# Node stage of a graph layer on one core: the residual term formed by GpSimd and copied into PSUM by ScalarE instead of transposed in by TensorE

## The chip, the cores and the metric

The kernel runs on one core of a Trainium2 chip. The metric is the device time of one execution in microseconds (us). The kernel before was timed three times: 1971.91, 1972.24 and 1974.71 us, median 1972.24.

Five engines are named in what follows: TensorE (PE, and PEld for its weight loads), VectorE (DVE), ScalarE (ACT), GpSimd (POOL) and SyncE (SP, which issues DMAs).

## The reference, cut to what matters

x has 50000 rows of 256, there are 12500 edges and 8 heads. The change lies in the part after the attention.

```python
h = maximum(layernorm(x), 0)                      # row by row
out = attention over the edges, of h              # other stages; their result + Wo_b is the table "agg"
out = layernorm(h + out, ln1_g, ln1_b)            # "zn * g1 + b1", zn without gain and shift
ffn = gelu(out @ ffn_w1 + ffn_b1) @ ffn_w2 + ffn_b2
out = layernorm(out + ffn, ln2_g, ln2_b)
return x + out
```

All is float32. Products of the feed-forward part are made from split operands: each factor is a high part (rounded to the fast matmul type f32r) and a low part (the rest), and three of the four products are summed.

## The kernel before

Four stages run one after the other: scores of the edges, softmax, messages, and the node stage (function `node_stage`), which is the one that changes. The node stage takes the rows in NG = 98 groups of GR = 512 rows, GT = 4 tiles of 128 rows each. KD = 2 halves of the 256 features, KF = 4 quarters of the 512 hidden features. Each engine has its program written out for all groups: a loop over `s` from -6 to NG, in which every engine does, in a fixed order, a part of the work of group s and parts of groups before and after it. Semaphores tie the engines together; an engine works strictly in its own order.

TensorE, step s: F, the first product, quarter by quarter (c = 0 to 3, six matmuls of 512 columns each, L904, f32r) into two PSUM banks in turn; then eight transposes of `ut` into the banks of Y (L912), which start the accumulation with the residual term; then eight transposes of `zn` of group s+1 into T (L923, T has two banks); then the second product, 48 matmuls of 256 columns (L931), into the same Y.

ScalarE, step s: `zn` of group s+1 (L819), gelu of each quarter from PSUM into `act_full` in SBUF (L850), its high part `act_hi` (L856), the first layer's normalisation `z` of group s+4 (L819), the high part `zt_hi` of T (L874, 1024 elements), and `ut = g1 * T + (b1 + fb2)` (L879, twice 512 elements).

VectorE, step s: for group s-1, once its second product is done, statistics of Y (L760, four), their aggregation (L763, four) and the centring of Y (L779, four); then `low_part(s, 0)` (L768: `act_lo = act_full - act_hi`), statistics of z of group s+2, `low_part` 1 and 2, the output of group s-1 (L797, four), `low_part` 3, `zt_lo` of group s+1 (L805), statistics of x of group s+5. In front of each aggregation stands `hold`: a wait for the statistics and an increment of another semaphore.

GpSimd, step s: the DMA that adds `agg` to z of group s+3 (L722) and one that adds a constant to x (L724), then the small scale factors of x (s+4), of y (s-1) and of z (s+2) (L707 to L715), each with a power (L711) of 128x4. SyncE loads x (L681) and stores the result (L687).

TensorE waits for: `lo_done` (all of `zt_lo` of its group) before F; `gelu_done` of quarter c-2 before F of quarter c; `ut_done` and `o_done` before L912; `zn_done`, `lo_done` and `ut_done` before L923; `glo_done` (the low part of quarter c) before quarter c of the second product.

Of the kernel before, what the change touches and what calls it, by code (L numbers as in the profile page):

```python
# [18 lines left out]
P = 128  # L19
KD = D // P  # L20
KF = F // P
# [584 lines left out]
def node_stage(nc, x, given, w1, w2, out, agg_dram):  # L606

    with ExitStack() as ctx:
# [15 lines left out]
        res_col = sb("d_res_col", [P, KD])  # L624
        ident = sb("d_ident", [P, P])
        mhalf = sb("d_mhalf", [P, GT])
        xt = [sb(f"d_x{r}", [P, GT, D]) for r in range(XR)]
        z = [sb(f"d_z{r}", [P, GT, D]) for r in range(ZR)]
        zn = [sb(f"d_zn{r}", [P, GT, D]) for r in range(2)]
        zt_hi, zt_lo = sb("d_zt_hi", [P, KD, GR], f32r), sb("d_zt_lo", [P, KD, GR], f32r)  # L630
        act_full = sb("d_act", [P, KF, GR])
        act_hi, act_lo = sb("d_act_hi", [P, KF, GR], f32r), sb("d_act_lo", [P, KF, GR], f32r)
        ut = sb("d_ut", [P, KD, GR])
        o = [sb(f"d_o{r}", [P, GT, D]) for r in range(2)]
        norm = {n: dict(stats=sb(f"d_stats_{n}", [P, NR, GT, 6]), mv=sb(f"d_mv_{n}", [P, NR, GT, 2]),
                        veps=sb(f"d_veps_{n}", [P, NR, GT]), rstd=sb(f"d_rstd_{n}", [P, NR, GT]),
                        nmean=sb(f"d_nmean_{n}", [P, NR, GT]), nmr=sb(f"d_nmr_{n}", [P, NR, GT]), stats_done=sem(f"d_stats_done_{n}"),
                        mv_done=sem(f"d_mv_done_{n}"), veps_done=sem(f"d_veps_done_{n}"),
                        rstd_done=sem(f"d_rstd_done_{n}"), nmr_done=sem(f"d_nmr_done_{n}")) for n in "xzy"}
# [3 lines left out]
        w_in, consts, prep, bias_ps = sem("d_w_in"), sem("d_consts"), sem("d_prep"), sem("d_bias_ps")  # L643
        x_in = [sem(f"d_x_in{r}") for r in range(XR)]
        b2_in = [sem(f"d_b2_in{r}") for r in range(XR)]
        agg_in = [sem(f"d_agg_in{r}") for r in range(ZR)]
        stored = [sem(f"d_stored{r}") for r in range(2)]
        h_done, zn_done = sem("d_h_done"), sem("d_zn_done")
        t_done, hi_done, lo_done = sem("d_t_done"), sem("d_hi_done"), sem("d_lo_done")
        f_done, gelu_done, ghi_done, glo_done = sem("d_f_done"), sem("d_gelu_done"), sem("d_ghi_done"), sem("d_glo_done")  # L650
        ut_done = sem("d_ut_done")
        ffn_done, centred, o_done = sem("d_ffn_done"), sem("d_centred"), sem("d_o_done")
        passed, pool_passed = sem("d_passed"), sem("d_pool_passed")
# [4 lines left out]
                   (res_col, v["fb2_col"]))  # L658
        N_IN = 16 * (2 + len(vectors))
        FIRST, LAST = -6, NG + 1  # L660
        PREP = 8

        def rows_of(table, g):

            at = g.times(GR) if g.i is not None or g.c < NG - 1 else N - GR
            return table[bass.ds(at, GR), :].rearrange("(p j) d -> p j d", j=GT)

        with nc.Block() as block:
            @block.sync
            def _(sp):  # L670
                sp.dma_start(w1_raw[:], w1.rearrange("(k p) n -> p k n", p=P)).then_inc(w_in, 16)
                sp.dma_start(w2_raw[:], w2.rearrange("(k p) n -> p k n", p=P)).then_inc(w_in, 16)
                for to, of in vectors:
                    sp.dma_start(to[:], of).then_inc(w_in, 16)  # L674

                def step(s):
                    g = s + 6
                    if g.exists(NG):
                        if g.after(XR):
                            sp.wait_ge(o_done, g.times(1, 1 - XR))  # L680
                        sp.dma_start(xt[g.c % XR][:], rows_of(x, g)).then_inc(x_in[g.c % XR], 16)  # L681
                    g = s + -1
                    if g.exists(NG):
                        sp.wait_ge(o_done, g.times(1, 1))
                        if g.i is None and g.c == NG - 1:
                            sp.wait_ge(stored[(g.c - 1) % 2], (g + -1).use(2, 16))
                        sp.dma_start(rows_of(out, g), o[g.c % 2][:]).then_inc(stored[g.c % 2], 16)  # L687
                for s in range(FIRST, LAST):
                    step(Step(s))
                for r in range(2):  # L690
                    sp.wait_ge(stored[r], 16 * ((NG + 1 - r) // 2))

            @block.gpsimd
            def _(pool):
                nc.gpsimd.memset(ident[:], 0.0).then_inc(consts, 1)
                nc.gpsimd.memset(mhalf[:], -0.5).then_inc(consts, 1)
                pool.wait_ge(consts, 2)
# [4 lines left out]
                def scales(n, g):  # L702

                    q, r = norm[n], g.c % NR
                    hold(pool, q["mv_done"], g.times(1, 1), pool_passed)
                    if n != "y":
                        nc.gpsimd.tensor_scalar(q["nmean"][:, r], q["mv"][:, r, :, 0], -1.0, 0.0, ALU.mult, ALU.add)  # L707
                    nc.gpsimd.tensor_scalar(q["veps"][:, r], q["mv"][:, r, :, 1], 1.0, LN_EPS, ALU.mult, ALU.add)\
                        .then_inc(q["veps_done"], 1)
                    pool.wait_ge(q["veps_done"], g.times(1, 1))  # L710
                    nc.gpsimd.tensor_tensor(q["rstd"][:, r], q["veps"][:, r], mhalf[:], ALU.pow)\  # L711
                        .then_inc(q["rstd_done"], 1)
                    if n != "y":
                        pool.wait_ge(q["rstd_done"], g.times(1, 1))
                        nc.gpsimd.tensor_tensor(q["nmr"][:, r], q["nmean"][:, r], q["rstd"][:, r], ALU.mult)\  # L715
                            .then_inc(q["nmr_done"], 1)

                def step(s):
                    g = s + 3
                    if g.exists(NG):  # L720
                        pool.wait_ge(h_done, g.times(1, 1))
                        pool.dma_start(z[g.c % ZR][:], rows_of(agg_dram, g), accum_op=ALU.add)\  # L722
                            .then_inc(agg_in[g.c % ZR], 16)
                        pool.dma_start(xt[g.c % XR][:], b2_wide[:], accum_op=ALU.add).then_inc(b2_in[g.c % XR], 16)  # L724
                    g = s + 4
                    if g.exists(NG):
                        scales("x", g)
                    g = s + -1
                    if g.exists(NG):
                        scales("y", g)  # L730
                    g = s + 2
                    if g.exists(NG):
                        scales("z", g)
                for s in range(FIRST, LAST):
                    step(Step(s))

            @block.vector
            def _(dve):
# [16 lines left out]
                done(nc.vector.tensor_tensor(res_col[:], res_col[:], b1_col[:], ALU.add))  # L755

                def statistics(name, g, t):
                    q, r = norm[name], g.c % NR
                    for j in range(GT):
                        nc.vector.bn_stats(q["stats"][:, r, j, :], t[:, j, :]).then_inc(q["stats_done"], 1)  # L760
                    hold(dve, q["stats_done"], g.times(GT, GT), passed)
                    for j in range(GT):
                        ins = nc.vector.bn_aggr(q["mv"][:, r, j, :], q["stats"][:, r, j, :])  # L763
                    ins.then_inc(q["mv_done"], 1)

                def low_part(s, c):
                    dve.wait_ge(ghi_done, s.times(KF, c + 1))
# [3 lines left out]
                def step(s):  # L771
                    y = s + -1
                    q, yr, yn = norm["y"], y.c % 2, y.c % NR
                    if y.exists(NG):
                        dve.wait_ge(ffn_done, y.times(1, 1))
                        statistics("y", y, Y[yr])
                        dve.wait_ge(q["mv_done"], y.times(1, 1))
                        for j in range(GT):
                            nc.vector.scalar_tensor_tensor(Y[yr][:, j, :], Y[yr][:, j, :], q["mv"][:, yn, j, 0:1],  # L779
                                                           g2_row[:], ALU.subtract, ALU.mult).then_inc(centred, 1)  # L780
                    if s.exists(NG):
                        low_part(s, 0)
                    g = s + 2
                    if g.exists(NG):
                        dve.wait_ge(agg_in[g.c % ZR], g.use(ZR, 16))
                        statistics("z", g, z[g.c % ZR])
                    if s.exists(NG):
                        low_part(s, 1)
                        low_part(s, 2)
                    if y.exists(NG):  # L790
                        dve.wait_ge(q["rstd_done"], y.times(1, 1))
                        dve.wait_ge(b2_in[y.c % XR], y.use(XR, 16))
                        dve.wait_ge(centred, y.times(GT, GT))
                        if y.after(2):
                            dve.wait_ge(stored[yr], (y + -2).use(2, 16))
                        for j in range(GT):
                            ins = nc.vector.scalar_tensor_tensor(o[yr][:, j, :], Y[yr][:, j, :], q["rstd"][:, yn, j:j + 1],  # L797
                                                                 xt[y.c % XR][:, j, :], ALU.mult, ALU.add)
                        ins.then_inc(o_done, 1)
                    if s.exists(NG):  # L800
                        low_part(s, 3)
# [194 lines left out]
```

## Time and profile before

The profiled execution took 1970.92 us, of which 1969.2 us lie between its first and its last instruction.

| | busy us | share of the span | instructions |
|---|---|---|---|
| PE | 1767.6 | 90% | 10564 |
| PEld | 1498.4 | 76% | 10564 |
| DVE | 1503.4 | 76% | 4348 |
| ACT | 1278.4 | 65% | 2290 |
| POOL | 1046.1 | 53% | 1645 |

The node stage takes the span from about 624 us on; its first F matmul starts at 672.36 us and the last instructions of group 97 end the execution. The profile cuts the span into 40 slices and gives each engine's busy tenths in them; the second row is TensorE's granted clock in tenths of full speed.

```profile
PE   0999999729892499999999999999999999999997
PEclk9999999959896699999999999999999999999999
```

From the fifteenth slice on PE is busy for nine tenths or more. Busy says that a matmul was under way, not that the engine was at its peak. The chain that ended last is followed back from the last instruction, and names at each step what released it.

```profile
PE 66%; DVE 1%; POOL 1%; DMA 0%; ACT 0%; issue 0%; SPq 0%; DVEq 0%; POOLq 0%; ACTq 0%
```

### The profile page before, as it was taken

Reading aid. Unit: us, or ns where it says so; the run is one execution under the profiler, and the core shown is the slowest. Engines: PE = TensorE matmul, PEld = TensorE weight load, DVE = VectorE, ACT = ScalarE, POOL = GpSimd, SP = SyncE. Lnnn points to the kernel's source line nnn. Section 1 sums busy time; section 2 is a strip of 40 time slices with the busy share of each in tenths; the row PEclk is TensorE's granted clock in tenths of the full one; section 3 lists DMA queues with packets and bytes.
Section 4 is the critical chain, followed back from the end, with each engine's and each line's share of the span. In section 5 each row is a group of like instructions: output and inputs, shape, how many; then the busy total and the mean of one; then the engine's idle time right before and its main releaser. Section 6 shows DMA issues by size and latency. Waiting matters only on the chain.

```text
span 1969.2 us, 32889 instructions
## 1 busy us (share of the span) xinstructions
PE 1767.6 (90%) x10564; PEld 1498.4 (76%) x10564; DVE 1503.4 (76%) x4348; ACT 1278.4 (65%) x2290; POOL 1046.1 (53%) x1645
## 2 busy tenths in 40 slices
PE   0999999729892499999999999999999999999997
PEld 0666666516561399999999999999999999999997
DVE  2554554357671599999999999999999999999986
ACT  1666666400000588888888888888888888888884
POOL 6777776006773555555555555555555555555541
PEclk9999999959896699999999999999999999999999
DMA  3677677402333667766776667666766676667651
GB/s 100 222 236 243 216 247 234 150 30 79 109 119 105 144 154 160 169 160 157 159 171 157 158 158 171 158 156 159 172 158 157 158 171 159 158 156 171 160 120 43
DMA packets 131718, 308.26 MB, mean 157 GB/s; under 512 B 13917, under 2 KB 67851, under 8 KB 131569
## 3 DMA queue, kind: packets, MB, share of 16 engines
q0 software_dynamic: 42624, 139.33, 33.2%
q1 hardware_dynamic: 36800, 114.52, 19.7%
q10 hardware_dynamic: 52144, 52.56, 8.4%
q8 instruction: 76, 1.25, 0.3%
q14 instruction: 74, 0.60, 0.1%
HBM read 139.98 MB, written 117.79 MB: 131 GB/s over the span
## 4 chain that ended last, share of the span: by engine, by line
PE 66%; DVE 1%; POOL 1%; DMA 0%; ACT 0%; issue 0%; SPq 0%; DVEq 0%; POOLq 0%; ACTq 0%
PE d_Y L931 29%; PE d_F L904 28%; PE d_Y L912 4%; PE d_T L923 4%; DMA d_res_col<-in_fb_col 0%; ACT d_z L819 0%; POOL d_rstd_x L711 0%; POOL d_x L724 0%; PE d_F L889 0%; SPq L674 0%; DVE d_Y L779 0%; DVE d_stats_y L760 0%; DVE d_stats_x L760 0%; POOL d_z L722 0%; DVE d_o L797 0%
## 5 line engine op out<-in xcount | busy, mean ns | idle before, releaser
L931 PE MATMUL d_Y<-d_w_hi,d_act_hi 128*128 128x256 f32 x1568 | 451.2, 288 | 0.0
L931 PE MATMUL d_Y<-d_w_lo,d_act_hi 128*128 128x256 f32 x1568 | 443.0, 283 | 0.0
L931 PE MATMUL d_Y<-d_w_hi,d_act_lo 128*128 128x256 f32 x1568 | 439.4, 280 | 0.0
L819 ACT ACTIVATE d_z<-d_x,d_nmr_x,d_rstd_x 128x256 f32<-128x256 f32 x392 | 223.9, 601 | 253.6 <-POOL d_nmr_x L715 253.6
L850 ACT ACTIVATE d_act<-d_F,d_fb_col 128x512 f32<-128x512 f32 x392 | 266.9, 681 | 145.1 <-PE d_F L904 144.9
L904 PE MATMUL d_F<-d_zt_hi,d_w_hi 128*128 128x512 f32 x784 | 311.8, 398 | 3.3 <-DVE d_zt_lo L805 3.3
L904 PE MATMUL d_F<-d_zt_lo,d_w_hi 128*128 128x512 f32 x784 | 311.6, 397 | 0.0
L904 PE MATMUL d_F<-d_zt_hi,d_w_lo 128*128 128x512 f32 x784 | 311.0, 397 | 0.0
L931 PEld LDWEIGHTS d_Y<-d_w_hi,d_act_lo 128*128 128x128 f32 x1568 | 298.4, 190 | 0.0
L931 PEld LDWEIGHTS d_Y<-d_w_hi,d_act_hi 128*128 128x128 f32 x1568 | 294.5, 188 | 0.0
L931 PEld LDWEIGHTS d_Y<-d_w_lo,d_act_hi 128*128 128x128 f32 x1568 | 293.3, 187 | 0.0
L768 DVE TENSOR_TENSOR d_act_lo<-d_act,d_act_hi 128x512 fp32r<-128x512 f32 x392 | 257.2, 676 | 6.3 <-ACT d_act_hi L856 6.3
L856 ACT ACTIVATE d_act_hi<-d_act 128x512 fp32r<-128x512 f32 x392 | 244.7, 624 | 0.3
L819 ACT ACTIVATE d_zn<-d_z,d_nmr_z,d_rstd_z 128x256 f32<-128x256 f32 x392 | 222.2, 593 | 0.0
L760 DVE BATCH_NORM_STATS2 d_stats_y<-d_Y 128x6 f32<-128x256 f32 x392 | 139.7, 419 | 79.3 <-PE d_Y L931 79.3
L879 ACT ACTIVATE d_ut<-d_T,d_res_col,d_g_col 128x512 f32<-128x512 f32 x196 | 142.0, 775 | 87.1 <-DVE d_zt_lo L805 87.1
L707 POOL TENSOR_SCALAR d_nmean_z<-d_mv_z 128x4 f32<-128x4 f32 x98 | 42.1, 430 | 276.0 <-DVE d_mv_z L763 276.0
L904 PEld LDWEIGHTS d_F<-d_zt_hi,d_w_lo 128*128 128x128 f32 x784 | 148.0, 189 | 36.1
L904 PEld LDWEIGHTS d_F<-d_zt_hi,d_w_hi 128*128 128x128 f32 x784 | 148.1, 189 | 35.6 <-DVE d_zt_lo L805 3.7
L904 PEld LDWEIGHTS d_F<-d_zt_lo,d_w_hi 128*128 128x128 f32 x784 | 148.0, 189 | 31.2
L779 DVE SCALAR_TENSOR_TENSOR d_Y<-d_Y,d_mv_y,d_g_row 128x256 f32<-128x256 f32 x392 | 163.3, 485 | 3.5
L722 POOL DMA_DIRECT2D d_z<-agg_scratch x98 | 91.2, 930 | 134.8 <-ACT d_z L819 134.8
(147 smaller groups left out, 3634.9 us busy)
## 6 DMA issues: line engine op xcount, KB each, us to landing
agg_scratch<-a_bias_row ACTq DMA_DIRECT2D x50, 1024.0 KB, 6.5
d_x<-in_x SPq DMA_DIRECT2D x98, 512.0 KB, 5.3
d_z<-agg_scratch POOLq DMA_DIRECT2D x98, 512.0 KB, 7.4
d_x<-d_b_wide POOLq DMA_DIRECT2D x98, 512.0 KB, 9.2
out<-d_o SPq DMA_DIRECT2D x98, 512.0 KB, 2.9
c_cont<-cont_scratch SPq DMA_DIRECT2D x25, 256.0 KB
a_xd<-in_x,a_idx_now POOLq DMA_INDIRECT x100, 6.1
a_xs<-in_x,a_idx_now POOLq DMA_INDIRECT x100, 2.9
```

Of the source, the lines that this page charges most:

```text
L722: pool.dma_start(z[g.c % ZR][:], rows_of(agg_dram, g), accum_op=ALU.add)\
L760: nc.vector.bn_stats(q["stats"][:, r, j, :], t[:, j, :]).then_inc(q["stats_done"], 1)
L768: nc.vector.tensor_tensor(act_lo[:, c, :], act_full[:, c, :], act_hi[:, c, :].bitcast(f32), ALU.subtract).then_inc(glo_done, 1)
L779: nc.vector.scalar_tensor_tensor(Y[yr][:, j, :], Y[yr][:, j, :], q["mv"][:, yn, j, 0:1], g2_row[:], ALU.subtract, ALU.mult).then_inc(centr ...
L819: return nc.scalar.activation(to[:, j, :], of[:, j, :], func, bias=q["nmr"][:, r, j:j + 1], scale=q["rstd"][:, r, j:j + 1])
L850: nc.scalar.activation(act_full[:, c, :], FF[:, c % 2, :], ACT.Gelu, bias=fb1_col[:, c:c + 1])\
L856: nc.scalar.activation(act_hi[:, c, :], act_full[:, c, :], ACT.Identity).then_inc(ghi_done, 1)
L879: nc.scalar.activation(ut[:, k, :], T[:, k, :], ACT.Identity, bias=res_col[:, k:k + 1], scale=g1_col[:, k:k + 1]).then_inc(ut_done, 1)
L904: ins = nc.tensor.matmul(FF[:, c % 2, :], w[:, k, c * P:(c + 1) * P], a[:, k, :], start=(k == 0 and p == 0), stop=(k == KD - 1 and p == 2))
L912: nc.tensor.matmul(out[:, j, k * P:(k + 1) * P], ut[:, k, j * P:(j + 1) * P], ident[:], is_transpose=True, start=(j % 2 == 0 and k == 0), ...
L923: ins = nc.tensor.transpose(T[:, k, j * P:(j + 1) * P], zn[g.c % 2][:, j, k * P:(k + 1) * P], ident[:])
L931: ins = nc.tensor.matmul(out[:, j, :], a[:, c, j * P:(j + 1) * P], w[:, c, :], start=False, stop=(c == KF - 1 and w is w2_lo), skip_group_ ...
```

## The change

All of it is in the node stage; nine points.

1. The residual term is made as rows, not as columns: GpSimd multiplies `zn` by the gain row into a new buffer `u` (one instruction of 1024 elements per partition and group), and ScalarE copies `u` into the two banks of Y (1024 elements). TensorE opens the Y banks once, ahead of the loop, with four f32 matmuls of 512 columns.
2. The constant row b1 + fb2 is added by four matmuls of 256 columns with a contraction over two rows (`ones` and `res`, high and low part). The eight transposes of `ut` and the two ScalarE instructions for it go.
3. gelu is written in place in its PSUM bank; `act_full` goes, and the high and the low part read PSUM.
4. F has three banks instead of two, and F of a quarter now waits for the low part (`glo_done`), on VectorE, of the quarter three turns before it: F of quarter 3 waits for `low_part(s, 0)`.
5. T has one bank instead of two: `zn` is transposed one half at a time. The first half stands between F and the second product, the second half behind quarter 1 of the second product, where it waits for `lo_done` of the first half. `zt_hi` and `zt_lo` are made half by half.
6. VectorE's order: y block, low 0, statistics of z and half of those of x, low 1, aggregation of z, the rest of x, low 2, aggregation of x, low half 0 of T, low 3, two tiles of the output, low half 1 of T, the other two tiles.
7. `hold` goes; each aggregation has its own wait for its own statistics.
8. GpSimd's order: scale factors of y first, then the DMAs, the multiply, and the factors of z and x together (128x8).
9. At the start three row vectors are loaded and combined; ScalarE waits for the opening of the Y banks.

Buffers and banks:

```diff
-        XR, ZR, NR = 8, 4, 4
+        XR, ZR, NR, FB = 8, 4, 4, 3
...
-        T, FF = psum("d_T", [P, KD, GR]), psum("d_F", [P, 2, GR])
+        T, FF = psum("d_T", [P, GR]), psum("d_F", [P, FB, GR])
```

GpSimd, the multiply:

```diff
+                    g = s + 1
+                    if there(g):
+                        pool.wait_ge(zn_done, g + 1)
+                        if g >= 2:
+                            pool.wait_ge(seeded, g - 1)
+                        nc.gpsimd.tensor_tensor(u[g % 2][:], zn[g % 2][:], wide(g1_row), ALU.mult).then_inc(u_done, 1)
```

VectorE, aggregation, low part and the end of its step:

```diff
-                    hold(dve, q["stats_done"], g.times(GT, GT), passed)
-                    for j in range(GT):
-                        ins = nc.vector.bn_aggr(q["mv"][:, r, j, :], q["stats"][:, r, j, :])
...
+                        for j in range(GT):
+                            dve.wait_ge(ystats_done, GT * y + j + 1)
+                            ins = nc.vector.bn_aggr(y_mv[:, yr, j, :], y_stats[:, yr, j, :])
+                        ins.then_inc(ymv_done, 1)
...
-                    nc.vector.tensor_tensor(act_lo[:, c, :], act_full[:, c, :], act_hi[:, c, :].bitcast(f32),
-                                            ALU.subtract).then_inc(glo_done, 1)
+                        nc.vector.tensor_tensor(act_lo[:, c, :], FF[:, (KF * s + c) % FB, :], act_hi[:, c, :].bitcast(f32),
+                                                ALU.subtract).then_inc(glo_done, 1)
...
+                    z_low_part(s + 1, 0)
+                    low_part(s, 3)
+                    output((0, 1))
+                    z_low_part(s + 1, 1)
+                    output((2, 3))
```

ScalarE:

```diff
+                            nc.scalar.activation(bank, bank, ACT.Gelu, bias=fb1_col[:, c:c + 1]).then_inc(gelu_done, 1)
...
                     high_part(0)
                     gelu(1)
                     norm_z((3,))
+                    if there(s):
+                        act.wait_ge(u_done, s + 1)
+                        if s >= 2:
+                            act.wait_ge(o_done, s - 1)
+                        nc.scalar.activation(Y[s % 2][:], u[s % 2][:], ACT.Identity).then_inc(seeded, 1)
                     high_part(1)
                     gelu(2)
-                    norm_x((0,))
                     high_part(2)
                     gelu(3)
-                    norm_x((1,))
+                    z_high_part(0)
                     high_part(3)
...
+                    norm_x((0, 1, 2))
+                    z_high_part(1)
+                    norm_x((3,))
```

TensorE:

```diff
+                for r in range(2):
+                    for j in range(0, GT, 2):
+                        ins = nc.tensor.matmul(Y[r][:, j:j + 2, :], ident[:], w2_raw[:, j:j + 2, :], start=True, stop=True)
+                ins.then_inc(y_open, 1)
...
+                            turn = KF * s + c
+                            if c == 0:
+                                pe.wait_ge(lo_done, KD * (s + 1))
+                            if turn >= FB:
+                                pe.wait_ge(glo_done, turn + 1 - FB)
...
+                    transposes(s + 1, 0)
+                    if there(s):
+                        pe.wait_ge(seeded, s + 1)
                         for j in range(GT):
-                            for k in range(KD):
-                                nc.tensor.matmul(out[:, j, k * P:(k + 1) * P], ut[:, k, j * P:(j + 1) * P], ident[:],
-                                                 is_transpose=True, start=(j % 2 == 0 and k == 0), stop=False,
-                                                 skip_group_check=True)
...
+                            nc.tensor.matmul(Y[s % 2][:, j, :], ones[:], res[:], start=False, stop=False, skip_group_check=True)
...
+                        if c == 1:
+                            transposes(s + 1, 1)
```

## Rows read from the trace of the kernel before

**Rows 1.** Window: length, busy (count) of PE, PEld, DVE, ACT, POOL, clock, DMA.

```profile
800.00:1300.00 500.00, 500.00 (x3359) 456.36 (x3359) 455.23 (x1412) 411.15 (x725) 260.92 (x459) 1.00 0.70 161
```

**Rows 2.** Chain that ended last, one period: start us, us, what.

```profile
1343.40 5.63 PE d_F L904 x24
1349.02 0.87 PE d_Y L912 x8
1349.90 0.87 PE d_T L923 x8
1350.77 5.75 PE d_Y L931 x48
```

**Rows 3.** Timeline of PE, same period: F's first matmuls of quarters 0 and 3.

```profile
1343.23 0.40 PE L904 MATMUL d_F<-d_zt_hi,d_w_hi 128*128 128x512 f32 x1
...
1347.45 0.40 PE L904 MATMUL d_F<-d_zt_hi,d_w_hi 128*128 128x512 f32 x1
```

**Rows 4.** Timeline of DVE, same period: start us, us, engine, line, instruction, count, [idle before].

```profile
1343.43 1.42 DVE L760 BATCH_NORM_STATS2 d_stats_y<-d_Y 128x6 f32<-128x256 f32 x4 [0.71 <-PE d_Y L931]
1345.00 0.38 DVE L763 BATCH_NORM_AGGREGATE d_mv_y<-d_stats_y 128x2 f32<-128x6 f32 x4
1345.41 1.67 DVE L779 SCALAR_TENSOR_TENSOR d_Y<-d_Y,d_mv_y,d_g_row 128x256 f32<-128x256 f32 x4
1346.99 0.68 DVE L768 TENSOR_TENSOR d_act_lo<-d_act,d_act_hi 128x512 fp32r<-128x512 f32 x1
1347.59 1.40 DVE L760 BATCH_NORM_STATS2 d_stats_z<-d_z 128x6 f32<-128x256 f32 x4
1349.13 0.38 DVE L763 BATCH_NORM_AGGREGATE d_mv_z<-d_stats_z 128x2 f32<-128x6 f32 x4
1349.43 1.26 DVE L768 TENSOR_TENSOR d_act_lo<-d_act,d_act_hi 128x512 fp32r<-128x512 f32 x2
...
1352.78 1.22 DVE L805 TENSOR_TENSOR d_zt_lo<-d_T,d_zt_hi 128x1024 fp32r<-128x1024 f32 x1
```

**Rows 5.** Chain that ended last, first group: VectorE releases TensorE.

```profile
671.08 1.24 DVE d_zt_lo L805
...
672.36 7.71 PE d_F L904 x24
```

**Rows 6.** Groups by form, all of the run: weight load of F, and f32 matmuls.

```profile
L904 PEld LDWEIGHTS d_F<-d_zt_hi,d_w_lo 128*128 128x128 f32 x784 | 148.0, 189 | 36.1
...
L538 PE MATMUL c_Y<-c_wo,c_total 128*128 128x256 f32 x400 | 104.8, 421 | 7.4 <-DVE c_total L567 7.3
```

**Rows 7.** Timeline of ACT, same period as rows 2.

```profile
1344.84 0.69 ACT L850 ACTIVATE d_act<-d_F,d_fb_col 128x512 f32<-128x512 f32 x1 [1.49 <-PE d_F L904]
...
1345.92 0.62 ACT L856 ACTIVATE d_act_hi<-d_act 128x512 fp32r<-128x512 f32 x1
...
1351.19 1.02 ACT L874 ACTIVATE d_zt_hi<-d_T 128x1024 fp32r<-128x1024 f32 x1
...
1354.03 1.45 ACT L879 ACTIVATE d_ut<-d_T,d_res_col,d_g_col 128x512 f32<-128x512 f32 x2 [0.84 <-DVE d_zt_lo L805]
```

**Rows 8.** Groups by form, POOL, all of the run.

```profile
L708 POOL TENSOR_SCALAR d_veps_z<-d_mv_z 128x4 f32<-128x4 f32 x98 | 52.0, 531 | 6.1
...
L199 POOL TENSOR_TENSOR a_rstd<-a_veps,a_mhalf 128x8 f32<-128x8 f32 x25 | 41.8, 1673 | 2.1
...
L708 POOL TENSOR_SCALAR d_veps_x<-d_mv_x 128x4 f32<-128x4 f32 x98 | 19.0, 194 | 6.2
...
L698 POOL TENSOR_SCALAR_AFFINE_SELECT d_ident<-d_ident 128x128 f32<-128x128 f32 x1 | 0.3, 288 | 0.1
```

**Rows 9.** DMA issues on the page: KB each, median us from issue to landing.

```profile
d_z<-agg_scratch POOLq DMA_DIRECT2D x98, 512.0 KB, 7.4
```

**Rows 10.** Chain that ended last, start of the node stage, and ACT's first instruction there.

```profile
646.26 0.17 DVE d_res_col L755
...
650.55 2.08 ACT d_z L819 x4
```

More of the change, by code:

```diff
@@ L657, in node_stage, with there, wide @@
                    (b2_wide, v["b2"].rearrange("o (j d) -> o j d", j=1).broadcast_to([P, GT, D])),
-                   (res_col, v["fb2_col"]))
+                   (g1_row, v["g1"].broadcast_to([P, D])), (res_row, v["b1"].broadcast_to([P, D])),
+                   (fb2_row, v["fb2"].broadcast_to([P, D])))
         N_IN = 16 * (2 + len(vectors))
         FIRST, LAST = -6, NG + 1
-        PREP = 8
+        PREP = 13
+        def there(g):
+            return 0 <= g < NG
+        def wide(row):
+            return row[:].rearrange("p (j d) -> p j d", j=1).broadcast_to([P, GT, D])
         def rows_of(table, g):
-            at = g.times(GR) if g.i is not None or g.c < NG - 1 else N - GR
+            at = g * GR if g < NG - 1 else N - GR
             return table[bass.ds(at, GR), :].rearrange("(p j) d -> p j d", j=GT)
@@ L674, in _ @@
                     sp.dma_start(to[:], of).then_inc(w_in, 16)
-                def step(s):
+                for s in range(FIRST, LAST):
                     g = s + 6
[L678 to L689, printed above, removed]
+                    if there(g):
+                        if g >= XR:
+                            sp.wait_ge(o_done, g + 1 - XR)
+                        sp.dma_start(xt[g % XR][:], rows_of(x, g)).then_inc(x_in[g % XR], 16)
+                    g = s - 1
+                    if there(g):
+                        sp.wait_ge(o_done, g + 1)
+                        if g == NG - 1:
+                            sp.wait_ge(stored[(g - 1) % 2], 16 * ((g - 1) // 2 + 1))
+                        sp.dma_start(rows_of(out, g), o[g % 2][:]).then_inc(stored[g % 2], 16)
                 for r in range(2):
@@ L810, in _ @@
-                for s in range(FIRST, LAST):
-                    step(Step(s))
+                done(nc.vector.tensor_tensor(res_row[:], res_row[:], fb2_row[:], ALU.add))
+                dve.wait_ge(consts, 6)
+                done(nc.vector.tensor_copy(ones[:], ones_raw[:]))
+                done(nc.vector.tensor_copy(res_hi[:], res_row[0:2, :]))
+                done(nc.vector.tensor_tensor(res_row[0:2, :], res_row[0:2, :], res_hi[:].bitcast(f32), ALU.subtract))
+                done(nc.vector.tensor_scalar(fb2_row[0:2, :], res_hi[:].bitcast(f32), pick[:, 0:1], None, ALU.mult))
@@ new lines, in _, with transposes @@
+                ins.then_inc(y_open, 1)
+                def transposes(g, k):
+                    if there(g):
+                        if k == 0:
+                            pe.wait_ge(zn_done, g + 1)
+                        if KD * g + k >= 1:
+                            pe.wait_ge(lo_done, KD * g + k)
+                        for j in range(GT):
+                            ins = nc.tensor.transpose(T[:, j * P:(j + 1) * P], zn[g % 2][:, j, k * P:(k + 1) * P], ident[:])
+                        ins.then_inc(t_done, 1)
@@ L926, in step @@
[L926 to L928 removed]
+                            nc.tensor.matmul(Y[s % 2][:, j, :], ones[:], res[:], start=False, stop=False, skip_group_check=True)
+                    for c in range(KF):
+                        if there(s):
+                            pe.wait_ge(glo_done, KF * s + c + 1)
                             for j in range(GT):
                                 for a, w in ((act_hi, w2_hi), (act_lo, w2_hi), (act_hi, w2_lo)):
[L931 removed]
+                                    ins = nc.tensor.matmul(Y[s % 2][:, j, :], a[:, c, j * P:(j + 1) * P], w[:, c, :],
```

312 lines of the change are left out of this document (150 added, 162 removed).

## Prediction

> **What bounds the kernel now.** I read first the windows of the steady state: in 500 us TensorE is busy for 500.00 at a granted clock of 1.00, its full 2.4 GHz, VectorE for 455, ScalarE for 411, GpSimd for 261 [rows 1]. Busy alone doesn't prove a bound, so next the chain that ended last: it runs through TensorE alone, and one period of it is F 5.63 us, eight transposes of `ut` 0.87, eight transposes of `zn` 0.87, second product 5.75, in sum 13.12 [rows 2]. In VectorE's timeline it sat idle 0.71 before its y block, waiting for TensorE [rows 4]. So TensorE sets the period and VectorE stands only 0.7 us behind. Of 98 groups, 97 periods count. What is worth a saving is read from the period, and what takes it away from the moments at which VectorE delivers; I therefore count from F's first matmul, 1343.23 = 0. F of quarter 3 then starts at 4.22 [rows 3].
>
> **TensorE's own work.** Eight transposes of `ut` go: -0.87 [rows 2]. Four matmuls of 256 columns come. Their nearest row is the second product, 5.75 / 48 = 0.12 each [rows 2], so +0.48. A contraction over two rows isn't in the trace; below, nothing can be cheaper than a transpose of half the columns, 0.87 / 8 = 0.11 each (0.43), above, an F matmul of twice the columns, 5.63 / 24 = 0.235 each (0.94). I take 0.48, the same column count and type. The transposes of `zn` are the same eight, in two parts of 0.43. If nothing else is late, the period is 13.12 - 0.87 + 0.48 = 12.73: -0.39 each, -38 us in 97.
>
> **The new wait.** F of quarter 3 now waits for `low_part(s, 0)`, and behind it in TensorE's order stands everything: transposes, residual, second product. VectorE makes that low part behind its y block. Before: y block from 0.20, low part from 3.76 to 4.44 (1346.99 to 1347.67) [rows 4]. TensorE wants it at 4.22. Unchanged, the chain would cost 0.22, plus the hop and the weight load. For the hop: `d_zt_lo` began at 671.08 and took 1.24, and the matmul that waited for it followed at 672.36, 0.04 later [rows 5]. A weight load takes 0.19 [rows 6], and can't run ahead of the wait. So F of quarter 3 would start at 4.48 to 4.67, a stall of 0.26 to 0.45: about all that the removed transposes give.
>
> But point 7 shortens the y block. The four statistics end at 1344.85 and the first aggregation begins at 1345.00; the plain wait behind the aggregations costs 0.03 (1345.38 to 1345.41) [rows 4]. So `hold` costs 0.15 where a wait costs 0.03, and it also held back the three aggregations whose statistics were done. Four aggregations take 0.38, the first three of them 0.22 to the start of the fourth. In the change three run while the last statistics finish, and only the fourth waits: it starts at 1.62 + 0.03, ends 0.16 later, and centring starts at 1.84, not 2.18. That is -0.34 at best. If the four waits cost 0.03 each it is -0.24. The low part then ends at 4.10 to 4.20. With 0.04 for the hop and 0 to 0.19 for the weights F of quarter 3 starts at 4.22 (not late) to 4.43: a stall of 0 to 0.21. I take 0.15, nearer the upper end, because the weight load of a waiting matmul is in the trace and its absence isn't. Low part 0 itself: one operand in PSUM, one in SBUF, as `d_zt_lo`, 1.22 for 1024 elements, against 1.26 for the two low parts of 512 in SBUF [rows 4]: no change. Period: 12.73 + 0.15 = 12.88.
>
> **What else could be late.** VectorE from low part 0 (start 3.52): steps of 0.60 (1346.99 to 1347.59), 0.33 for each statistic (1.40 less the 0.41 of one, in three), 0.30 for four aggregations (1349.13 to 1349.43) [rows 4]. Six statistics 1.98, low 1 0.60, aggregation 0.30, two statistics 0.66, low 2 0.60, aggregation 0.30: low half 0 of T starts at 8.56 and ends at 9.24. TensorE reaches the second half's transposes at 0.15 + 5.63 + 0.43 + 0.48 + 2.87 = 9.56. Slack about 0.3, and 0.1 with the weights. The rest of VectorE's step (low 3, two output pairs of 0.83, low half 1) ends near 12.1, before 13.08, so it doesn't bound. `hold` gone twice more is -0.2 in it; the split T is one more instruction, +0.1.
>
> ScalarE: `ut` goes, -1.45 less an overlap; the seed of 1024 elements comes. Writing to PSUM isn't in the trace: below 1.02 as `d_zt_hi`, above 1.24 as two high parts [rows 7]; I take 1.0. gelu 0 starts at 1.61 and high part 0 ends at 3.31 [rows 7], before VectorE asks at 3.5. Seed at 4.3 to 5.3, high 1 done at 5.9, asked at 6.1; the seed is asked by TensorE at 6.2. high 2 has gelu 2 just ahead of it and waits for its end, +0.1: done at 7.1, asked at 7.6. ScalarE's sum falls by 0.3 and it had 2.3 idle (1.49 + 0.84) [rows 7]. So zero. It would cost if the seed were over 0.2 longer.
>
> GpSimd: the multiply isn't in the trace. Below it, VectorE's 1.22 for two operands of 1024 [rows 4]; above, the slope of the select of 128 elements, 0.288 [rows 8], times 8 for 1024 elements and times 2 for two operands, 4.6. I take 2.3. It starts at 5.3, behind y's factors and two DMA issues, and ends at 7.6, or 9.9. The factors of z and x are asked for at 8.6; the joint power of 128x8 took 1.67 [rows 8], so they are ready at 11.1, or 12.4, and ScalarE needs them about two tiles (1.1) before gelu 0 at 14.5. Hidden at both ends. The Trainium skill speaks against such a placement (GPSIMD Engine Reference, section 4.1, Engine selection: elementwise work with two inputs is about twice as slow on GpSimd); from its figure of 4497 ns for 2048 elements an estimate is 2.25 us, which no row here shows.
>
> Queues moved past: the agg DMA now is issued near 3.5 and lands 7.4 later [rows 9], asked for a period later; the result is stored from 12.1 and the load of x behind it in SP's queue has more than a period. Zero.
>
> **Start and end.** VectorE's preparation ended at 646.43, ScalarE began at 650.55 [rows 10]. Two more DMA issues (+1), about 2 more of preparation in VectorE, and four f32 matmuls of 512 columns that ScalarE waits for: 0.42 for 256 [rows 6] makes 3.4 for four, twice that at the lower clock, against the 4.1 that ScalarE waited anyway: 0 to 2.7. The ramp may gain back 2 to 3, since x's factors of a group are no longer behind the DMA issues of the next. Sum 0 to +6, taken +2.5. The last group is unchanged.
>
> **Sum.** -0.87 + 0.48 + 0.15 = -0.24 a period; 97 x 0.24 = 23; 1970.9 - 23 + 2.5 = 1950. The profiled execution is 1.3 under the median, so 1951.
>
> **The rivals.**
> A, the forecast, a stall of 0.05 to 0.21: 1942 to 1958. 42%.
> B, no stall: -38 + 2.5, about 1937; if the weights cost nothing and waits are free. For it: TensorE has waits ahead of L912, L923 and L931, and the chain has no gap at any of them [rows 2]. 25%.
> C, the stall eats the gain (0.3 to 0.45, the y block as long as before): 97 x 0.39 is given back, 1966 to 1980. 13%.
> D, slower: every wait in front of an aggregation costs w, in place of one `hold`. Four stand ahead of low part 0, eight more ahead of low half 0 of T, which then makes TensorE wait a second time. Stalls are 0.15 + 4w + (8w - 0.3). Past w = 0.045 they exceed 0.39; at 0.10 the period is 13.78 and the time about 2037; at `hold`'s 0.15 [rows 4] some 90 more. Against it: the two low parts each have a wait between them and take 1.26 together, no gap [rows 4]. With it I count that the multiply holds VectorE's reads, which at 2.3 would pass the slack of 0.3 and cost up to 190 us. `d_veps_z` took 0.531 beside the low parts and `d_veps_x`, the same work, 0.194 [rows 8]: the two engines do hinder each other. The Trainium skill (SBUF — State Buffer, Who interferes with whom) says that VectorE contends with GpSimd's reads only with two SBUF inputs; in the change the low parts read PSUM, and by that rule this half of D can't happen, and the row agrees. 20%.
>
> **How the numbers follow.** A, B and C hold 80%: 1934 (B with nothing lost at the start) to 1982. A measurement here can tell about 0.2%, 4 us. Faster by more: A, B and none of C, 67%. Within: part of C, 9%. Slower: the rest of C and D, 24%.
>
> **What would show it.** A: TensorE waits once a period, before F of quarter 3, for `d_act_lo`, under 0.25 us; no record of a wait before the second half's transposes; mv_y begins before stats_y end; period near 12.88. B: 12.73 and no such wait. C and D: the period at 13.1 or over; in D gaps between the aggregations or a wait of d_T for `d_zt_lo`. I am wrong most easily in the 0.34 of the y block and in the two-row matmul, if it isn't 0.12.

## The result, and the profile after

The change makes the kernel slower: 1988.07 us median (1987.03 to 1990.82, four runs) against 1972.16 us, a ratio of 1.008 with a 95% interval of 1.0062 to 1.0097. The forecast was 1951 with a range of 1934 to 1982. The profiled execution has a span of 1985.3 us, 16.1 more than before.

The first part of the page of the changed kernel: busy us, share of the span, instructions.

```profile
PE 1786.4 (90%) x10180; PEld 1463.0 (74%) x10180; DVE 1488.1 (75%) x4451; ACT 1239.1 (62%) x2290; POOL 1127.7 (57%) x1366
```

The window that answers to [rows 1], in the same columns:

```profile
800.00:1300.00 500.00, 500.00 (x3177) 437.20 (x3176) 444.26 (x1440) 394.27 (x721) 290.37 (x342) 1.00 0.68 160
```

TensorE is still busy throughout at its full clock, so a slower clock doesn't explain the loss, and this view shows no idle TensorE, though the list of waits below does. VectorE and ScalarE have less to do than before. The chain that ended last, one period of the changed kernel (start us, us, what), answers to [rows 2]:

```profile
1341.14 5.76 PE d_F L957 x24
1346.90 0.44 PE d_T L944 x4
1347.34 0.67 PE d_Y L964 x4
1348.00 3.08 PE d_Y L970 x24
1351.08 0.44 PE d_T L944 x4
1351.51 2.87 PE d_Y L970 x24
1354.38 3.75 PE d_F L957 x16
```

The sum of the first six is 13.26; over 83 periods, from the y block at 706.02 to the one at 1804.35, the mean is 13.233 us, against 13.117 over 84 periods before (700.73 to 1802.52). Two pieces are as the sum had them: the transposes, twice 0.44, and the second half of the second product, 2.87. Three are longer: F by 0.13, the two-row matmuls (L964) by 0.19 over the 0.48 assumed, and the half of the second product that follows them by 0.21.

How the two-row matmuls look in TensorE's own timelines, first its matmuls, then its weight loads:

```profile
1346.51 0.39 PE L957 MATMUL d_F<-d_zt_hi,d_w_lo 128*128 128x512 f32 x1
1346.74 0.60 PE L944 MATMUL d_T<-d_ident,d_zn 128*128 128x128 f32 x4
1347.27 0.73 PE L964 MATMUL d_Y<-d_res,d_ones 2*128 2x256 f32 x4
1347.93 0.39 PE L970 MATMUL d_Y<-d_w_hi,d_act_hi 128*128 128x256 f32 x1
1348.16 0.28 PE L970 MATMUL d_Y<-d_w_hi,d_act_lo 128*128 128x256 f32 x1
```

```profile
1346.51 0.59 PEld L944 LDWEIGHTS d_T<-d_ident,d_zn 128*128 128x128 f32 x4
1347.26 0.53 PEld L964 LDWEIGHTS d_Y<-d_res,d_ones 2*128 2x128 f32 x4 [0.17 <-issue]
1347.93 0.19 PEld L970 LDWEIGHTS d_Y<-d_w_hi,d_act_hi 128*128 128x128 f32 x1
1348.04 0.19 PEld L970 LDWEIGHTS d_Y<-d_w_hi,d_act_lo 128*128 128x128 f32 x1
```

A weight load normally runs ahead of its matmul: the transposes' first load starts at 1346.51 and their first matmul at 1346.74. The load of L964 starts at 1347.26 and its matmul at 1347.27, and the same happens on the way out, 1347.93 and 1347.93. Ahead of the first the weight loader stood idle for 0.17 us with nothing that the profile shows to wait for. In the chain that is 0.19 at the two-row matmuls and 0.21 behind them.

VectorE's timeline, which answers to [rows 4]:

```profile
1341.18 1.43 DVE L813 BATCH_NORM_STATS2 d_y_stats<-d_Y 128x6 f32<-128x256 f32 x4 [0.76 <-PE d_Y L970]
1342.52 0.36 DVE L816 BATCH_NORM_AGGREGATE d_y_mv<-d_y_stats 128x2 f32<-128x6 f32 x4
1342.92 1.67 DVE L820 SCALAR_TENSOR_TENSOR d_Y<-d_Y,d_y_mv,d_g_row 128x256 f32<-128x256 f32 x4
1344.50 0.68 DVE L783 TENSOR_TENSOR d_act_lo<-d_F,d_act_hi 128x512 fp32r<-128x512 f32 x1
...
1349.45 0.66 DVE L789 TENSOR_TENSOR d_zt_lo<-d_T,d_zt_hi 128x512 fp32r<-128x512 f32 x1
```

F's first matmul is at 1340.98 here. The aggregations begin at 1342.52, before the statistics end at 1342.61, and low part 0 starts 3.52 after F and ends at 4.20. The waits of the steady state, 83 periods (engine, line, released by: us in total, times, longest):

```profile
ACT d_F L889 <- PE d_F L957: 184.9, 84, 2.2
...
DVE d_zt_lo L789 <- ACT d_zt_hi L899: 57.0, 83, 0.7
...
PEld d_F L957 <- DVE d_act_lo L783: 26.0, 83, 0.3
PEld d_Y L964 <- issue: 13.9, 83, 0.2
```

TensorE waits once a period for VectorE, for `d_act_lo`, and never for `d_zt_lo`. The 26.0 us are those of the weight loader, 0.31 a period. F is only 0.13 longer, so by the difference matmuls already under way cover 0.18 of it.

The multiply on GpSimd: line, form, count | busy us, mean ns.

```profile
L735 POOL TENSOR_TENSOR d_u<-d_zn,d_g_row 128x1024 f32<-128x1024 f32 x98 | 291.1, 2970 | 7.5 <-ACT d_zn L869 7.5
```

Where the 16.1 us of the span are: the period's 0.116 in 97 periods is 11.3; the stage's start, from its first DMA issue to F's first matmul, is 54.00 us (622.95 to 676.95) in place of 48.07 (624.29 to 672.36), 5.9; the earlier stages, which nothing touches, ended 1.3 sooner in this execution. 11.3 + 5.9 - 1.3 = 15.9, and 0.2 stays unexplained.

### The profile page after: what moved, and what is told of

Read it like the earlier page. It is cut to its first block, busy times and chain, and to the rows that moved or that the text cites. A ratio compares the mean times of both kernels' runs of the same rounds, so it can differ in the third digit from the quotient of the medians.

```text
span 1985.3 us, 31164 instructions
## 1 busy us (share of the span) xinstructions
PE 1786.4 (90%) x10180; PEld 1463.0 (74%) x10180; DVE 1488.1 (75%) x4451; ACT 1239.1 (62%) x2290; POOL 1127.7 (57%) x1366
## 4 chain that ended last, share of the span: by engine, by line
PE 66%; DVE 1%; DMA 1%; ACT 0%; SPq 0%; issue 0%; POOL 0%; DVEq 0%; ACTq 0%; POOLq 0%
PE d_Y L970 29%; PE d_F L957 29%; PE d_T L944 4%; PE d_Y L964 3%; DMA d_fb_row<-in_fb 1%; PE d_Y L934 0%; DMA d_z<-agg_scratch 0%; PE d_F L927 0%; SPq L685 0%; ACT d_zn L869 0%; ACT d_z L880 0%; POOL d_zx_rstd L748 0%; DVE d_y_stats L813 0%; DVE d_zt_lo L789 0%; DVE d_zx_stats L826 0%
## 5 line engine op out<-in xcount | busy, mean ns | idle before, releaser
L889 ACT ACTIVATE d_F<-d_F,d_fb_col 128x512 f32<-128x512 f32 x392 | 259.2, 661 | 217.8 <-PE d_F L957 217.7
L880 ACT ACTIVATE d_z<-d_x,d_zx_nmr,d_zx_rstd 128x256 f32<-128x256 f32 x392 | 213.9, 608 | 251.3 <-PE d_Y L934 249.0
L735 POOL TENSOR_TENSOR d_u<-d_zn,d_g_row 128x1024 f32<-128x1024 f32 x98 | 291.1, 2970 | 7.5 <-ACT d_zn L869 7.5
L783 DVE TENSOR_TENSOR d_act_lo<-d_F,d_act_hi 128x512 fp32r<-128x512 f32 x392 | 265.7, 678 | 11.1 <-ACT d_act_hi L894 11.1
L894 ACT ACTIVATE d_act_hi<-d_F 128x512 fp32r<-128x512 f32 x392 | 234.1, 597 | 3.2
L869 ACT ACTIVATE d_zn<-d_z,d_zx_nmr,d_zx_rstd 128x256 f32<-128x256 f32 x392 | 223.0, 594 | 5.8 <-POOL d_zx_nmr L751 5.7
L813 DVE BATCH_NORM_STATS2 d_y_stats<-d_Y 128x6 f32<-128x256 f32 x392 | 139.7, 419 | 77.8 <-PE d_Y L970 77.8
L789 DVE TENSOR_TENSOR d_zt_lo<-d_T,d_zt_hi 128x512 fp32r<-128x512 f32 x196 | 132.4, 675 | 73.8 <-ACT d_zt_hi L899 73.8
L805 DVE SCALAR_TENSOR_TENSOR d_o<-d_Y,d_y_rstd,d_x 128x256 f32<-128x256 f32 x392 | 169.6, 475 | 0.0
L748 POOL TENSOR_TENSOR d_zx_rstd<-d_zx_veps,d_mhalf 128x8 f32<-128x8 f32 (+1 forms) x101 | 164.1, 1625 | 8.4
```

The costliest lines, as they stand in the source:

```text
L735: nc.gpsimd.tensor_tensor(u[g % 2][:], zn[g % 2][:], wide(g1_row), ALU.mult).then_inc(u_done, 1)
L748: nc.gpsimd.tensor_tensor(zx_rstd[:, r, part], zx_veps[:, r, part], mhalf[:, part], ALU.pow)\
L783: nc.vector.tensor_tensor(act_lo[:, c, :], FF[:, (KF * s + c) % FB, :], act_hi[:, c, :].bitcast(f32), ALU.subtract).then_inc(glo_done, 1)
L789: nc.vector.tensor_tensor(zt_lo[:, k, :], T[:], zt_hi[:, k, :].bitcast(f32), ALU.subtract)\
L813: nc.vector.bn_stats(y_stats[:, yr, j, :], Y[yr][:, j, :]).then_inc(ystats_done, 1)
L869: ins = nc.scalar.activation(zn[gz % 2][:, j, :], z[gz % ZR][:, j, :], ACT.Identity, bias=zx_nmr[:, at % NR, 0, j:j + 1], scale=zx_rstd[:, ...
```

## The experiments

**Theory T**: a matmul whose contraction covers few rows uses TensorE's array in another arrangement; going into it and out of it costs 0.38 us, however many such matmuls stand together. The arrangement itself isn't seen in a trace; the runs test the cost, where it falls and on what it depends. **Rival S**: the gap belongs to the wait for ScalarE's seed (its copy of `u` into the Y banks), or to the seeded bank. **Rival P**: each of the two-row matmuls is slow. **Rival F**: the gain was lost to the wait of F's quarter 3. Periods below are means over 79 to 90 of them, from one y block to another, in the profiled execution. A time given without the word median is that of a single execution; several executions of one kernel lay within 5 us of each other.

### e1: the same matmuls, 128 rows high

```diff
-        ones, ones_raw, pick = sb("d_ones", [2, P], f32r), sb("d_ones_raw", [2, P]), sb("d_pick", [2, 2])
+        ones, ones_raw, pick = sb("d_ones", [128, P], f32r), sb("d_ones_raw", [128, P]), sb("d_pick", [128, 2])
```

`res` and `res_hi` are made as high, and what prepares them takes all rows; rows 2 and up of `res` are zero.

> The changed kernel with ones and res made 128 rows high, the rows beyond the first two of res being zero; same result, same four matmuls of 256 columns. The changed kernel's period is 13.24 us. Theory T (the two-row matmuls use the array in another arrangement, and going into and out of it empties the array; 0.86 us for the four with what follows, in place of 0.48): the period falls by 0.38 to 12.86, the time to 1988 - 97 x 0.38 = 1951 us, faster than the kernel before. Rival S (the gap at these matmuls is the wait for ScalarE's seed of Y, or the seeded bank): no change, 1988. Rival F (the wait of F's quarter 3 for the low part ate the gain): no change either, 1988.

Measured: 1952.8 us median (1951.99 to 1954.83), ratio to the kernel before 0.9902 (0.9885 to 0.9918); period 12.850. The chain that ended last, one period:

```profile
1344.36 0.44 PE d_T L944 x4
1344.80 0.48 PE d_Y L964 x4
1345.27 2.88 PE d_Y L970 x24
1348.15 0.44 PE d_T L944 x4
1348.59 2.88 PE d_Y L970 x24
```

0.67 became 0.48 and 3.08 became 2.88; the other pieces of the chain stayed within 0.01. 126 rows of zeros are worth 35 us. Seed, bank and wait are as they were, so S falls, and F falls as the main cause: the wait for `d_act_lo` is still there.

### e2: without the constant row

```diff
-                        for j in range(GT):
-                            nc.tensor.matmul(Y[s % 2][:, j, :], ones[:], res[:], start=False, stop=False, skip_group_check=True)
```

> The changed kernel without the four matmuls of the constant row; it leaves out b1 + fb2 in the residual. Theory T and rival P (each of the four is slow by itself): 0.86 us go, and TensorE then comes to the second half's transposes at 9.06 after F's start where VectorE has them ready at 9.2 to 9.3, so a wait of 0.1 to 0.2 appears there: period 12.5 to 12.6, time about 1922. Rival S: 0.48 go, the gap stays ahead of the second product, period 12.8, time 1945.

Measured: 1921.77 us, period 12.550, so 0.68 less. In the chain the second half's transposes take 0.63 in place of 0.44, and the list of waits (us in total, times, longest) has the new one:

```profile
1343.79 0.63 PE d_T L944 x4
1344.41 2.87 PE d_Y L968 x24
1347.28 5.76 PE d_F L957 x24
```

```profile
PEld d_T L944 <- DVE d_zt_lo L789: 13.6, 80, 0.2
```

The four matmuls with their surcharge cost 0.68 + 0.19 = 0.87: to the hundredth what the eight removed transposes of `ut` cost [rows 2]. So on TensorE the exchange of one for the other gained nothing.

### e3: eight two-row matmuls

```diff
+                        for j in range(GT):
+                            nc.tensor.matmul(Y[s % 2][:, j, :], ones[:], res[:], start=False, stop=False, skip_group_check=True)
```

> The changed kernel with eight two-row matmuls in a row in place of four (the constant row is added twice). Theory T (the surcharge of 0.38 is for going in and out, once): +0.48 a period, 13.72, time 2035. Rival P (each two-row matmul costs 0.21): +0.86 a period, 14.1, time 2071.

Measured: 2035.95 us, period 13.713, +0.480. The chain has the first four at 0.66 and the four added (L966) at 0.48:

```profile
1345.85 0.66 PE d_Y L964 x4
1346.51 0.48 PE d_Y L966 x4
```

Rival P falls: inside the group each costs 0.12; the surcharge is paid once.

### e4 and e12: 64 and 96 rows

As e1, with 64 rows (e4) and 96 rows (e12) in place of 128:

```diff
-        ones, ones_raw, pick = sb("d_ones", [2, P], f32r), sb("d_ones_raw", [2, P]), sb("d_pick", [2, 2])
+        ones, ones_raw, pick = sb("d_ones", [64, P], f32r), sb("d_ones_raw", [64, P]), sb("d_pick", [64, 2])
```

> The changed kernel with ones and res 64 rows high, the rows beyond the first two of res being zero. Theory T says only that a part of the array is another arrangement than the whole; if half of it counts as a part: 13.24, 1988; if only a quarter does, 12.86 and 1951. Rivals S and F: 1988. It tells apart where the surcharge begins, together with e1.

> The changed kernel with ones and res 96 rows high. Two and 64 rows gave 1988 and 1989, 128 rows 1953. If the surcharge of theory T falls away with more than half of the rows: period 12.86, time 1953. If it needs all 128: 13.24, 1988.

Measured: 64 rows 1989.11 us, period 13.235; 96 rows 1951.55 us, period 12.836. Weight loads by form, 64 rows first, then 96 (the last two columns: busy us, mean ns | idle before):

```profile
L964 PEld LDWEIGHTS d_Y<-d_res,d_ones 64*128 64x128 f32 x304 | 40.4, 185 | 12.7 <-issue 12.7
```

```profile
L964 PEld LDWEIGHTS d_Y<-d_res,d_ones 96*128 96x128 f32 x312 | 42.3, 192 | 0.0
```

The idle time "issue" ahead of the weight loads is there with 2 and 64 rows and gone with 96 and 128. The boundary is between 64 and 96 rows; where exactly isn't shown.

### e8 and e9: the same in the kernel before

Four matmuls on zeros, with 2 rows (e8) and 128 rows (e9), are put between the transposes of `zn` and the second product of the kernel before, which has no seed.

```diff
+                        for j in range(GT):
+                            nc.tensor.matmul(out[:, j, :], nil_a[:], nil_b[:], start=False, stop=False, skip_group_check=True)
```

> The kernel BEFORE with four added matmuls of two rows and 256 columns, whose operands are zeros, between its transposes of zn and its second product; nothing else is changed, no seed, no wait. Period before 13.12. Theory T: +0.86 to 0.9 a period, 13.98, time 1972 + 85 = 2057. Rivals S and F (the gap belongs to the seed or to other waits): +0.48, 13.60, time 2019.

> The same as the run before it with 128 rows of zeros: four added matmuls of 128 rows and 256 columns in the kernel BEFORE. Both theories: +0.48 a period, 13.60, time 2019. The difference of the two runs is the surcharge by itself, 0.38 x 98 = 37 us by theory T, none by the rivals.

Measured: e8 2058.16 us, period 13.980, +0.863; e9 2020.88 us, period 13.593, +0.476. The difference is 0.387 a period and 37.3 us, without anything else of the change. The chains, two pieces of e8 and then one of e9:

```profile
1341.55 0.66 PE d_Y L931 x4
1342.21 5.95 PE d_Y L936 x48
```

```profile
1351.18 0.48 PE d_Y L931 x4
```

In e8 the four take 0.66 in place of 0.48, and the whole second product behind them 5.95 in place of 5.75 [rows 2]: the same two places as in the changed kernel. The disputed cost is measured by itself, and theory T stands as to cost, place and dependence on the rows. That it is the arrangement of the array which changes is an account that fits, not something a trace shows.

### e5: low part 0 one instruction earlier

VectorE does low part 0 between the third and the fourth centring.

```diff
-                        for j in range(GT):
-                            nc.vector.scalar_tensor_tensor(Y[yr][:, j, :], ...
-                    low_part(s, 0)
+                        centre(range(3))
+                    low_part(s, 0)
+                    if there(y):
+                        centre(range(3, GT))
```

> The changed kernel with low part 0 moved one instruction ahead in VectorE's order, between the third and the fourth centring. It was ready 0.13 us a period too late for F's quarter 3; a centring is 0.39 to 0.42 long, and high part 0 is done 3.26 after F's start, so the low part now starts at 3.31 in place of 3.52. Stall 0.13 goes to 0: period 13.11, time 1988 - 12 = 1976. A theory that the stall is the main loss (rival F) would expect 1951 or less.

Measured: 1975.87 us median (1974.15 to 1977.62), ratio to the kernel before 1.0015 (1.0006 to 1.0025); period 13.081, -0.152. F is back to 5.61 in the chain, and TensorE's wait for `d_act_lo` is gone from the list:

```profile
1350.79 5.61 PE d_F L962 x24
```

The stall was worth 0.15 us a period, 12 us, and was not the main loss. With it gone and the surcharge left, the change is within 0.2% of the kernel before.

### e11: ScalarE's wait for the Y banks at its first seed

```diff
-                act.wait_ge(y_open, 1)
...
+                        if s == 0:
+                            act.wait_ge(y_open, 1)
```

> The changed kernel with one thing changed: ScalarE waits for the opening of the Y banks at its first seed, not at the head of its program. In the changed kernel the stage's first DMA issue to F's first matmul took 54.00 us, in the kernel before 48.07. Expected 51 (as in e7, 51.14), so 3 us less, 1985; the rest of the start is the added preparation. If it stays at 54, something else delays the start.

Measured: 1986.52 us, which by itself is too near the changed kernel's 1987.03 to 1990.82 to settle 3 us. The interval settles it: from the stage's first DMA issue to F's first matmul 51.19 us (625.71 to 676.90), 2.8 less. In the seven traces with the wait at the head it is 52.9 to 54.3, in e7 and e11 51.1 and 51.2. In the changed kernel the opening matmuls stand on the chain for 6.76 us:

```profile
648.89 6.76 PE d_Y L934 x8
655.65 0.03 ACTq L878
655.68 0.05 issue
655.73 2.08 ACT d_z L880 x4
```

The other 3.1 us of the longer start remain with this wait moved, and the chains of this trace and of the kernel before divide them. TensorE's first matmuls of the stage begin 14.94 us behind the first DMA issue in place of 13.08, 1.9 more, with three vectors loaded in place of one. VectorE's preparation ends 26.16 behind it in place of 22.14, another 2.2 more. The way from there to F's first matmul is 0.9 shorter. e10 leaves out five of the added instructions of the preparation (its order is changed too), and its start is 49.12, 2.1 less than in this run.

### e7: the three together

The edits of e1, e5 and e11 in one kernel, as their diffs above show them.

> The changed kernel with full-height ones and res (as e1), low part 0 one instruction earlier (as e5), and ScalarE's wait for the opening of the Y banks moved from the head of its program to its first seed. Sum by theory T: period 12.73; start 4 us shorter, as the changed kernel's first F matmul came at 676.95 in place of 672.36: 1988 - 97 x 0.51 - 4 = 1935. If the parts don't add, VectorE's low half 0 of T (ready 9.2 after F's start, asked at 9.4) is where a new wait shows.

Measured: 1939.24 us median (1936.59 to 1940.05), ratio 0.9827 (0.981 to 0.9843); period 12.734, as the sum had it. The 4 us over the expectation are ahead of the steady state: the start was 51.14 us, 2.9 shorter and not 4, and the earlier stages, which nothing touches, ended 4.9 later in this execution than in the changed kernel's (627.89 against 622.95). No wait of TensorE is left in the steady state.

### e10: the constant row by GpSimd

```diff
+                    g = s + 1
+                    if there(g):
+                        pool.wait_ge(u_mul, g + 1)
+                        nc.gpsimd.tensor_tensor(u[g % 2][:], u[g % 2][:], wide(res_row), ALU.add).then_inc(u_done, 1)
...
                     high_part(2)
+                    z_high_part(0)
                     gelu(3)
-                    z_high_part(0)
...
-                    z_low_part(s + 1, 0)
...
+                    z_low_part(s + 1, 0)
                     low_part(s, 2)
```

> The constant row added by GpSimd to u with a second instruction of 1024 elements (behind the scale factors of z and x), no constant row on TensorE; low part 0 one instruction earlier and ScalarE's wait for the Y banks at its first seed, as in e7; ScalarE makes the first high half of T ahead of gelu 3 and VectorE its low half ahead of low part 2. Same result as the reference. TensorE's work is 12.25 a period (12.73 less 0.48). If a GpSimd instruction with two operands in SBUF (3.0 us each) doesn't hold VectorE, and GpSimd's sum (1.3 + 1.9 + 3.0 + 2.5 + 3.0 = 11.7 of 12.25) is hidden: period 12.25 to 12.35, time 1939 - 97 x 0.45 = 1895. If it holds VectorE or GpSimd's chain ends last, the period is over 12.6 and VectorE's instructions beside the multiply are longer than their 0.68 and 0.41.

Measured: 1887.47 us median (1885.44 to 1887.88), ratio to the kernel before 0.9565 (0.9549 to 0.9581); period 12.232, just under the expected 12.25 to 12.35. Against e7 that is 52 us, 2.7%; the rest of the gain is that of the other edits. By form in the steady state, GpSimd's two large instructions and VectorE's low part beside them:

```profile
L735 POOL TENSOR_TENSOR d_u<-d_zn,d_g_row 128x1024 f32<-128x1024 f32 x82 | 247.7, 3020 | 0.0
L756 POOL TENSOR_TENSOR d_u<-d_u,d_res_row 128x1024 f32<-128x1024 f32 x82 | 196.2, 2392 | 0.0
```

```profile
L782 DVE TENSOR_TENSOR d_act_lo<-d_F,d_act_hi 128x512 fp32r<-128x512 f32 x327 | 220.6, 675 | 6.6
```

VectorE's instructions keep their length with GpSimd at work on two operands twice a period: the low part's mean is 675 ns, and was 676 in the kernel before. So the second half of rival D is ruled out here, where no VectorE instruction beside GpSimd's two reads two large operands from SBUF. TensorE waits for nobody, VectorE is idle 0.36 a period and GpSimd 1.8, so little more is to be had behind TensorE before VectorE binds. The instruction that added the row costs 2.4 where 3.0 had been taken; the multiply's 3.0 begins while the second DMA is still being issued, and it ends 2.4 after that issue (1343.07 to 1346.10, the issue to 1343.67).

## Why the prediction was wrong, point by point

**The bound** was right: TensorE set the period before and sets it after.

**"I take 0.48, the same column count and type"** is the step that failed: it is the term for the four two-row matmuls in the sum of TensorE's work. The nearest row was chosen by columns; the row count, the one thing in which the new matmul had no neighbour in the trace, was waved through. It measured 0.86 to 0.87 with its way in and out (e2, e8), 0.38 over, and so gave back all of the 0.87 that the removed transposes gained. The upper bound of 0.94 did contain it, so by my own rule of taking a value between ends by the nearest row, the range should have had this end: 97 x (0.94 - 0.48) is 45 us above 1951, 1996, and the range stopped at 1982. The bound was written down and then lost on the way to the range and to the rivals; none of the four was about it. The 24% for a slower kernel rested on rivals C and D, and neither is what happened.

The Trainium skill has this rule (TensorEngine Tiling (Array Packing), Tiling Modes, Key Properties): a change of the tiling mode, not just of the tile, drains TensorE. The case agrees, with 0.38 us for the two changes of a group. The Trainium skill lists, under Tiling Modes, Available Configurations on the same page, arrangements with 32, 64 and 128 rows, and that 64 rows pay (e4) and 96 don't (e12) agrees with that too. This rule spoke against the change, and the prediction didn't weigh it.

**The new wait** was right in place and nearly in size: a wait for `d_act_lo` ahead of F's quarter 3 in every period, 0.13 in the chain and 0.15 when removed (e5), 0.15 forecast. Low part 0 starts at 3.52, as in the working with a shorter y block: the centring starts 1.74 after the statistics in place of 1.98 [rows 4], 0.24 less, the lower of the two values given for it. The sign named for A, a wait under 0.25, holds for F's 0.13, not for the weight loader's 0.31. Rival B is out, since there is a stall. C wanted a stall of 0.3 to 0.45 and a y block as long as before; neither is there. D isn't there either: no second wait, and four aggregations with a wait each take 0.36 where they took 0.38. D's last figure is also worked out wrongly: by its own formula the stalls at 0.15 are 1.65, which is 0.60 and so 58 us above those at 0.10, not 90.

**What else could be late**: nothing was. `d_zt_lo` half 0 started at 8.47 (8.56 forecast), and TensorE reached its transposes at 10.1, later than the 9.56 forecast. The seed took 1.03. The multiply took 3.0 and not 2.3, inside its bounds and hidden as forecast.

**Start**: +5.9, against 0 to 6 forecast and 2.5 taken. By the chains the loads add 1.5 (1 forecast), the preparation 2.2 (2 forecast), and ScalarE's wait for the opening matmuls 2.8 (0 to 2.7 forecast); these ran for 6.76 us at a granted clock of 0.56 (window 648 to 656), the figure for the lower clock. The gain of 2 to 3 in the ramp was mis-sized: from ScalarE's first normalisation to F's first matmul it is 21.22 in place of 21.81, 0.6.

**The sum with measured terms**: -0.87 + 0.48 + 0.38 + 0.13 = +0.12 a period, 11.6 in 97; with 5.9 for the start 17.5. The medians differ by 15.9, the profiled executions by 16.1, and in these the earlier stages ended 1.3 sooner.

**The likeliest time** failed by one term; the other terms would have given 1951, and e1, which mends that term alone, measured 1952.8 with the start and the stall as they are. That it comes so near is in part luck: the start was 3.4 us longer than taken, and the period of e1, 12.850, 0.03 shorter than the 12.88 forecast, which is 3 us.

## What to carry to other kernels

When a new instruction differs from its nearest row in one property, that property has to be priced at both ends and carried into the range, even if the work looks smaller. In this kernel a small contraction between full ones cost 0.38 us a group more than its columns say: fill it with zeros to full height, as in e1, or let an engine with idle time do the work, as in e10. A wait added on an engine whose order is tight is worth a look at which instruction of its releaser can be moved one place ahead.

## What the runs showed of the hardware that I had not expected

Four matmuls of 256 columns between full-height ones cost 0.86 to 0.87 us with a contraction over 2 rows, 0.48 in the chain over 96 and 128, and 64 rows gave the period of 2 rows (13.235 against 13.233). Eight in a row cost 0.48 more than four: the surcharge of 0.38 us belongs to the change and not to the matmul. It shows in the trace as 0.17 us of idle weight loader with no releaser, and as a first weight load that starts with its matmul and not ahead of it.

GpSimd's instructions on 1024 elements with two operands in SBUF took 3.0 us (the multiply) and 2.4 (the addition of e10). They didn't lengthen VectorE's low parts, which read one operand from PSUM. The epsilon step of the scale factors took 0.197 in the changed kernel, where for z it had taken 0.531 beside the low parts with both operands in SBUF [rows 8]:

```profile
L745 POOL TENSOR_SCALAR d_zx_veps<-d_zx_mv 128x8 f32<-128x8 f32 x95 | 18.7, 197 | 6.0
```

That the operand in PSUM is the reason is argued from what runs beside the step; no run changes it alone.
